# Four equal stages with 2 KB rows, the last t of the third and fourth in two parts, low parts on DVE

## The reference

```python
h = jax.nn.sigmoid(jnp.einsum('bts,st->bs', x, W1) + b1)
return h @ W2.T + b2
```

## Time and profile before

| what | before |
|---|---|
| median of 3 runs | 311.82 us |
| the profiled execution | 311.89 us |
| its span | 310.1 us |
| PE busy | 257.8 us (83%) |
| DVE busy | 246.4 us (79%) |
| POOL busy | 215.2 us (69%) |
| ACT busy | 50.9 us (16%) |
| loads and stores | 109.48 MB, mean 353 GB/s |

### The profile page before, as it was taken

One profiled execution on the slowest core, in us unless ns is written; L12 is line 12 of the kernel. 1 busy time (PEld: TensorE's weight loads), 2 busy tenths in 40 slices (PEclk: granted clock), 3 DMA queues, 4 the chain that ended last, 5 costly groups with the idle time before them and its releaser, 6 DMA issues.

```text
span 310.1 us, 4779 instructions
## 1 busy us (share of the span) xinstructions
PE 257.8 (83%) x1761; PEld 220.0 (71%) x1761; DVE 246.4 (79%) x368; ACT 50.9 (16%) x85; POOL 215.2 (69%) x125
## 2 busy tenths in 40 slices
PE   0947678648888999999579999937999988999894
PEld 0846677647766888889468887835888885888783
DVE  0729899829998978889977987877878898798865
ACT  4211223203253100100420000040101104000120
POOL 3119676626379999995799977479988848999000
PEclk9979999959999999999999999999999999999999
DMA  7999999999999999999999999999999999999007
GB/s 223 398 390 385 387 385 386 402 387 388 385 387 384 387 386 388 386 385 384 373 374 374 385 381 381 381 385 373 373 373 373 370 359 340 339 349 332 29 2 272
DMA packets 67675, 109.48 MB, mean 353 GB/s; under 512 B 3642, under 2 KB 40514, under 8 KB 67652
## 3 DMA queue, kind: packets, MB, share of 16 engines
q1 hardware_dynamic: 67056, 107.06, 96.8%
q10 hardware_dynamic: 596, 2.11, 1.7%
HBM read 104.97 MB, written 4.19 MB: 352 GB/s over the span
## 4 chain that ended last, share of the span: by engine, by line
PE 51%; DMA 31%; DVE 7%; issue 5%; ACT 3%; SPq 1%; DVEq 0%; ACTq 0%
DMA ring<-in_r_x 31%; PE xbank L232 25%; PE pbank L301 20%; DVE acc L354 4%; PE xbank L332 3%; ACT h L431 2%; DVE w_lo L361 2%; ACT h_hi L456 1%; PE pbank L291 1%; PE pbank L332 1%; PE pbank L261 0%; DVE acc L352 0%; ACT L431 0%; SPq L195 0%; SPq L201 0%
## 5 line engine op out<-in xcount | busy, mean ns | idle before, releaser
L354 DVE SCALAR_TENSOR_TENSOR acc<-xbank,w,acc 128x512 f32<-128x512 f32 x280 | 200.0, 746 | 41.1 <-PE xbank L232 35.6
L232 PE MATMUL xbank<-ident,ring 128*128 128x128 f32 x1184 | 171.5, 279 | 44.2 <-DMA ring<-in_r_x 36.0
L232 PEld LDWEIGHTS xbank<-ident,ring 128*128 128x128 f32 x1184 | 142.2, 144 | 75.7 <-issue 27.9
L485 POOL TENSOR_TENSOR nat<-nat,w1all 128x768 f32<-128x768 f32 (+2 forms) x56 | 107.2, 1916 | 60.6 <-DMA nat<-in_r_x 47.1
L495 POOL TENSOR_TENSOR nat<-nat 128x768 f32<-128x768 f32 (+2 forms) x46 | 87.8, 1908 | 3.6
L301 PE MATMUL pbank<-w_hi,h_hi 128*128 128x512 f32 x112 | 48.2, 431 | 0.3 <-ACT h_hi L456 0.2
L301 PE MATMUL pbank<-w_lo,h_hi 128*128 128x512 f32 x112 | 48.3, 432 | 0.0
L301 PE MATMUL pbank<-w_hi,h_lo 128*128 128x512 f32 x112 | 40.5, 431 | 0.0
L431 ACT ACTIVATE h<-acc,b1col 128x512 f32<-128x512 f32 (+1 forms) x22 | 12.5, 599 | 96.1 <-DVE acc L354 64.0
L443 ACT COPY y<-pbank 128x512 f32<-128x512 f32 x16 | 9.4, 587 | 79.4 <-PE pbank L301 79.4
L301 PEld LDWEIGHTS pbank<-w_hi,h_hi 128*128 128x128 f32 x112 | 21.3, 191 | 1.4 <-ACT h_hi L456 1.0
(11 more groups left out here) (37 smaller groups left out, 93.1 us busy)
## 6 DMA issues: line engine op xcount, KB each, us to landing
ring<-in_r_x SPq DMA_DIRECT2D x38, 1024.0 KB, 13.4
ring<-in_r_x SPq DMA_DIRECT2D x36, 768.0 KB, 11.1
nat<-in_r_x SPq DMA_DIRECT2D x20, 512.0 KB, 13.1
nat<-in_r_x SPq DMA_DIRECT2D x24, 384.0 KB, 11.5
ring<-in_r_x SPq DMA_DIRECT2D x18, 512.0 KB, 7.8
y<-in_L_rec_W SPq DMA_DIRECT2D x2, 2048.0 KB, 14.9
nat<-in_r_x SPq DMA_DIRECT2D x12, 256.0 KB, 8.7
out_y<-y ACTq DMA_DIRECT2D x4, 512.0 KB, 6.6
```

The source lines that it names most:

```text
L232: mm = pe.transpose(xbank[u % XBANKS][:, j * P:(j + 1) * P], tile, ident[:, :])
L354: nc.vector.scalar_tensor_tensor(out=total, in0=bank, scalar=weight, in1=total, op0=ALU.mult, op1=ALU.add).then_inc(unit_added, 1)
L485: nc.gpsimd.tensor_tensor(slot, slot, row, ALU.mult).then_inc(nat_weighed, 1)
```

## The change

`STAGES` has four stages of four chunks each, so that every load has rows of 2 KB. The pools are 4, 6, 6, 6. In the third stage the last 6 t, and in the fourth the last 10 t, come in two parts of rows: first row tiles 0 and 1 of all of those t, then row tiles 2 and 3 of all of them. Such a half load has 512 KB; two share a slot of the ring, and a half unit has two transposes and is 128 x 256 for DVE. The "n" units of these stages come in halves too. When the first part is done, its sums are complete for half of the rows, and their sigmoid, high and low parts are made while the second part is turned. For the fourth stage, the product of the first two row tiles (4 outs) begins beside the turns of the second part, and after the last turn there are 12 steps left of it and then four outs of 12 matmuls, out by out. `steps_due` counts steps over the whole kernel by STRETCHES, in proportion to tiles turned. DVE makes the low parts in place of POOL, at four places (every second unit) after each stage and each first part. ACT makes each half's sigmoids after the outs due by then were kept, and issues its stores two tiles at a time.

```diff
 STAGES = (
-    (0, 0, 4, 4, (2, 3, 5, 7, 9, 11, 13, 15, 17, 18), "keep"),
-    (0, 4, 4, 6, (0, 2, 3, 5, 6, 8, 9, 11, 12, 14, 15, 17), "last"),
-    (4, 0, 3, 6, (0, 2, 3, 5, 6, 8, 9, 11, 12, 14, 15, 17), "keep"),
-    (4, 3, 3, 6, (0, 2, 3, 5, 6, 8, 9, 11, 12, 14, 15, 17), "add"),
-    (4, 6, 2, 6, (0, 2, 3, 5, 6, 8, 9, 11, 12, 13), "last"),
+    (0, 0, 4, 0, (2, 3, 5, 7, 9, 11, 13, 15, 17, 18), "keep"),
+    (0, 4, 6, 0, (0, 2, 3, 5, 6, 8, 9, 11, 12, 14, 15, 17), "last"),
+    (4, 0, 6, 6, (0, 2, 3, 5, 6, 8, 9, 11, 12, 14, 18, 20, 21, 23), "keep"),
+    (4, 4, 6, 10, (1, 3, 4, 6, 7, 9, 11, 13), "last"),
 )
+CUT = 2
+NC = 4
...
+    loads = [[(t, 0, JT) for t in range(pools[i], T - splits[i])] for i in range(NS)]
+    for i in range(NS):
+        loads[i] += [(t, *half) for half in halves[i] for t in range(T - splits[i], T) if splits[i]]
...
+        for t, row, n in loads[i]:
+            if t == T - 2:
+                order += [("n", 0, c, row, n) for c in range(NC)]
+            order += [("x", t, c, row, n) for c in range(NC)]
...
+        AHEAD = 16
+        LATE = 8
+        HEAD = OH * CUT * steps_of(LAST)
+        STRETCHES = (
+            (OUTS * steps_of(0), first_unit[1] + 2 * NC, first_unit[1] + len(units[1]) * 4 // 5),
+            (OUTS * steps_of(1), first_unit[2] + 2 * NC, part_end(2) + NC),
+            (AHEAD, part_end(2) + 2 * NC, first_unit[3]),
+            (OUTS * steps_of(2) - AHEAD - LATE, first_unit[3], part_end(3)),
+            (LATE, part_end(3), part_end(3) + 2 * NC),
+            (HEAD - REST, part_end(3) + 2 * NC, UNITS),
+        )
...
-                    q = item_of[i, pools[i] + at]
-                    if q >= RING:
-                        sp.wait_ge(unit_turned, item_end[q - RING] + 1)
-                    sp.dma_start(ring[:, q % RING, :, :n * P],
+                    use, sub, _ = held[i, t, row]
+                    if use >= RING and sub == 0:
+                        sp.wait_ge(unit_turned, use_end[use - RING] + 1)
+                    sp.dma_start(ring[:, use % RING, sub * n:(sub + 1) * n, :],
...
+                bank, total = xbank[u % XBANKS][:, :n * P], acc[:, c, row * P:(row + n) * P]
...
+            def low_part(i, p):
+                c, row, n = sums[i][p]
+                rows = slice(row * P, (row + n) * P)
+                dve.wait_ge(h_hi_ready, first_sum[i] + p + 1)
+                nc.vector.tensor_tensor(h_lo[:, c, rows], h[:, c, rows], h_hi[:, c, rows].bitcast(F32),
+                                        ALU.subtract).then_inc(h_lo_ready, 1)
...
+            for n in range(OH * CUT, OUTS):
+                j, cols = out_half(n)
+                bank = xbank[(UNITS + n - OH * CUT) % XBANKS]
+                pe.wait_ge(unit_added, UNITS - XBANKS + n - OH * CUT + 1)
+                for c in range(NC):
                     if n % OH == 0:
-                        pe.wait_ge(tail_lo, c * JT + j + 1)
+                        pe.wait_ge(tail_lo, sum_of(LAST, c, j) - TAIL + 1)
...
+                    if u in lows:
+                        low_part(*lows[u])
...
-            def low_parts(i):
-                for c in range(chunks[i]):
-                    pool.wait_ge(h_hi_ready, first_h[i] + c + 1)
```

More of the change, by code:

```diff
@@ L58, in rec_kernel @@
     UNITS = sum(len(o) for o in units)
-    first_h = [sum(chunks[:i]) for i in range(NS)]
+    sums = [[(c, *half) for half in halves[i] for c in range(NC)] for i in range(NS)]
+    sums[LAST] = [(c, 0, CUT) for c in range(NC)] + [(c, j, 1) for j in range(CUT, JT) for c in range(NC)]
+    first_sum = [sum(len(o) for o in sums[:i]) for i in range(NS)]
+    TAIL = NC
     OUTS = OH * JT
@@ L155, in steps_of, with part_end, steps_due, steps_to @@
         def steps_of(i):
[L157 to L172, removed]
+            return 3 * NC + (fate[i] == "keep")
+        def part_end(i):
+            return first_unit[i] + max(v for v, u in enumerate(units[i]) if u[3] == 0) + 1
+        AHEAD = 16
[9 more added lines that the diff above has]
+        )
+        tiles_to = [0]
+        for order in units:
+            for unit in order:
+                tiles_to.append(tiles_to[-1] + unit[4])
+        def steps_due(u):
+            due = 0
+            for steps, a, b in STRETCHES:
+                if u >= a:
+                    due += -(-steps * (tiles_to[min(u + 1, b)] - tiles_to[a]) // (tiles_to[b] - tiles_to[a]))
+            return due
+        def steps_to(outs):
+            return sum(steps_of(g // OUTS) for g in range(outs))
+        def out_end(g):
+            i, n = divmod(g, OUTS)
+            if any(n == OH * row for row, _ in halves[i]):
+                return steps_to(g + 1) + 2 * NC + (fate[i] == "keep")
+            return steps_to(g + 1)
+        def outs_due(u):
+            return sum(out_end(g) <= steps_due(u) for g in range((NS - 1) * OUTS + OH * CUT))
         EARLY, SETN = 1 + NK0, 1 + 2 * NK
@@ L185, in _ @@
             m = 0
-            for i, (j0, c0, n, _, places, _) in enumerate(STAGES):
-                for at in range(T - pools[i]):
+            for i, (j0, c0, _, _, places, _) in enumerate(STAGES):
+                for at, (t, row, n) in enumerate(loads[i]):
                     if at in places:
@@ L218, in turn_unit @@
                 u = first_unit[i] + v
-                kind, t, c = units[i][v]
+                kind, t, c, row, n = units[i][v]
                 if u >= XBANKS:
@@ L431, in sigmoid @@
+            def sigmoid(i, p):
+                c, row, n = sums[i][p]
+                rows = slice(row * P, (row + n) * P)
+                act.wait_ge(unit_added, sum_end(i, p))
                 nc.scalar.activation(h[:, c, rows], acc[:, c, rows], ACT.Sigmoid,
                                      bias=b1col[:, bass.ds(STAGES[i][1] + c, 1)]).then_inc(h_ready, 1)
+                if i < LAST or p < TAIL:
+                    act.wait_ge(h_ready, first_sum[i] + p + 1)
+                    nc.scalar.copy(h_hi[:, c, rows], h[:, c, rows]).then_inc(h_hi_ready, 1)
@@ L444, in _ @@
[L444 to L459 removed]
+                for half, (row, n) in enumerate(halves[i]):
+                    if i == 2 and half == 0:
+                        store_tile(0)
+                        store_tile(1)
+                    if i == 3 and half == 0:
+                        store_tile(2)
+                        store_tile(3)
+                    part = [p for p, s in enumerate(sums[i]) if row <= s[1] < row + n]
+                    outs = outs_due(sum_end(i, part[0]) - 1)
+                    for g in range(kept, outs):
+                        if fate[g // OUTS] == "keep":
+                            keep_out(g // OUTS, g % OUTS)
+                    kept = outs
+                    if i > 0:
+                        act.wait_ge(h_lo_ready, min(first_sum[i], first_sum[LAST]))
+                        act.wait_ge(out_summed, OUTS * (i - 1) + OH * (row + n))
+                    for p in part:
+                        sigmoid(i, p)
```

251 lines of the change are left out of this document (124 added, 127 removed).

## The result

The changed kernel takes 314.07 us (median of 4 runs, 313.76 to 318.29) against 311.78 us (4 runs): 0.7% slower by the medians. The ratio of the mean times is 1.010, with a 95% interval of 1.0069 to 1.0131; the one run of 318.29 us raises the ratio and widens its interval. The profiled execution took 314.37 us, with a span of 312.5.

The account below looks back on a forecast made before the run. Loads and PE were both taken as near their bound. Landing at 262.9 plus 29.9 of PE work gave the last turn at 292.9; 18.0 of tail made span 310.9, time 312.6 us, own range 311.5 to 313.8, whole range 309.9 to 315.5.

Parts of the forecast that it names:

- rival B: On PE, a half unit with one step takes 0.50 us, not 0.466: time 314.7; chance 0.22.
- wrong altogether: Sign: GB/s well under 386 before 280 us, or PE idle on h_hi or h_lo at the second part's start.
- landing of t = 19: Last stage's sixth half load, the last with a POOL load ahead of it, lands at 262.9 us.
- edit (1): DVE's extra work: 72 more units 8.6 us, 20 low parts 8.8 us, mostly under the loads outside the last part.
- edit 5: Last stage's ring holds 5 MiB, not 2.5; PE may lag some 11 us, so no gap in the loads.
- Rival D: Store cost beside reads moves the landings 1 us each way: last turn as much later, only 0.8 us earlier.
- rival A: On PE, half unit plus step takes 0.38 us, not 0.466, and DVE decides: time 309.9; chance 0.24.
- rival C: DVE's half units cost full duration, 0.480 us for 256 columns, not 0.39: time 316.4; chance 0.10.
- The tail: After the last turn: 18.0 us against 19.2 before, as PE's 1.2 us gap goes; 4.07 from last add to end.
- The stage turns (3): At a stage's turn, DVE's first multiply waits for its chunk's sigmoid as before; the loads cover it.
- SP's number of loads (4): SP issues 90 ring loads and 44 for POOL, before 92 and 56: zero cost.
- POOL (2): POOL loses 14 low parts, 17.7 us, and isn't late with its 44 parts: zero cost.

Follow-up runs that it names:

- e1: Changed kernel with 16 of its 20 low parts made by POOL, the last four still on DVE: 312.80 us, 1.003 to the kernel before.
- e2: Kernel before the change with only its 14 low parts moved from POOL to DVE: 312.16 us, 1.0009 to the kernel before.
- e3: Changed kernel with POOL's instructions 16 of each 512 columns wide, most work on its sums left out: 312.81 us, 1.0031 to the kernel before.
- e8: Changed kernel with 16 low parts on POOL and the third stage in one part, its product wholly in the last stage: 314.66 us.
- e9: Changed kernel with all low parts on POOL, third-stage steps earlier, and the last stage's last 8 t in two parts, not 10: 312.55 us.
- e11: Changed kernel with all low parts on POOL, third-stage steps earlier, and 12 of the last stage's t in two parts, not 10: 310.54 us.
- e10: Changed kernel with the low part as h times a constant, one SBUF input in place of two: 314.74 us, one run.

## Why the prediction came out as it did

The forecast was 312.6, slower by 0.25%; measured were 314.07, slower by 0.7%. The direction was right and the size a third. The forecast's own range ended at 313.8, and the measured time lies between it and rival B's 314.7, though B didn't come about. What did was the prediction's own sign of "wrong altogether", slices well under 386 GB/s ahead of 280 us, to which it gave 0.04. That the time is inside the whole range, 309.9 to 315.5, is therefore partly luck. The miss can be put beside the sum:

| term | forecast | changed kernel | e1 |
|---|---|---|---|
| landing of t = 19 | 262.9 | 266.25 | 264.78 |
| from PE's start on it to the last turn | 29.9 | 29.1 | 29.15 |
| last turn to the end of the span | 18.0 | 17.0 | 17.0 |
| span | 310.9 | 312.5 | 311.1 |

In both traces 13 steps follow the last turn, where the sum has 12, so 0.23 us of the third row belongs to the second; like for like PE's part was 0.5 us too long in the sum and the tail 1.2. In e1 these 1.8 us cancel a landing that is 1.9 us late: its total is right by luck, and the changed kernel's would have missed by 3.4 us without them.

- **The step that was mis-sized is edit (1), the low parts.** I took 0.60 and 0.33 us from start to start from rows in which POOL is idle (the 128-column piece at the end) or an input is in PSUM. Measured were 1665 and 1079 ns in duration, 26.3 us in all, where the sum had 8.8. I said that they lie under the loads outside the last part. In the kernel before they cost no time (e2), and in the changed one they made the hole: it is gone when they are (e1) and when POOL's instructions are short (e3).
- **"I expect no gap in the loads" (edit 5) was wrong.** I looked only at the slots of the ring. But the load for POOL waits for the last "n" units and holds the ring loads behind it, for 11.1 us here. The long low parts and the hole behind them are worth 1.3 us by e1 and e3. That this load's place has a part in it is read from the trace; another place for it was not tried.
- **The landing was 1.9 us late without the hole too.** In e1 the 27th load landed 0.3 us late already (issued at 97.30, landed at 110.2). From there to 264.78 the stream ran at 388 GB/s, no slower than in the sum, and so moved some 57.2 MiB (an estimate from rate and time) where the sum counts 56.5. So it is not the rate that was wrong but what had to move before that landing; whose bytes the 0.7 MiB are isn't settled. Rival D allowed 1 us.
- **PE's work behind the landing held.** In the changed kernel a half unit with one step takes 0.45 us (the starts of two transposes at 283.34 and 283.79), against 0.466 in the sum: neither rival A (0.38) nor B (0.50). The turn-and-step view of PE:

```profile
283.34 0.38 PE L303 MATMUL xbank<-ident,ring 128*128 128x128 f32 x2
283.47 0.48 PE L375 MATMUL pbank<-w_lo,h_hi 128*128 128x512 f32 x1
283.79 0.38 PE L303 MATMUL xbank<-ident,ring 128*128 128x128 f32 x2
```

- **DVE's half units held** (rival C fell): eight in 3.22 us with 475 ns for one are 0.39 from start to start. Of the two rules of the Trainium skill that the prediction cites (VectorE: DVE Perf Modes, the section on the errata and "The DRAIN you can't avoid"), the trace agrees with the fixed part of each small tile (2 x 0.39 is 0.12 more than 0.66) and not with the wait for an empty pipe.
- **The tail held but for the last store.** The gap before the product went. From the last add's start to the end are 3.1 us where I kept 4.07: the last adds, and so the last stores, are now 2.7 us apart, while before all eight stores were issued within 5.1 us. That the one explains the other is argued, not tried.
- **The stage turns (3) and SP's number of loads (4)** cost nothing that e1 shows. Nor does POOL (2), even with 16 low parts given back to it.

## What to carry to other kernels

Before an elementwise instruction is moved to DVE, look at what POOL does at that moment and whether the instruction has an input in PSUM: beside POOL's 2.4 us instructions, one without took two to three times its time, and rows with POOL idle don't show it. A faster load stream moves the bound to whatever work may only begin late; here the splits that let steps start earlier gained more than their fixed parts cost (e8, e9, e11), though why was read and not tried. A schedule edit is to be tried after the stall ahead of it is gone: the same 15 steps moved cost 2.0 us with the hole and gained 0.7 without.

## What the runs showed of the hardware

The low part, an f32 instruction of DVE from SBUF to SBUF, was held beside POOL's 128 x 1024 instructions with two inputs and with one (e10): it took up to 2.6 us where the subtraction takes 0.41 (256 columns) or 0.68 (512) undisturbed. When it meets one, it ends a fixed time after it, 0.55 us for 512 columns and 0.28 for 256, and about half of that with one input, so the two take turns and don't share. Instructions with one input in PSUM don't change (L421's kind 679 ns before and after, L423's 746 and 742). POOL's weighing grew too, from 2382 to 2413 ns on average, and the one begun at 96.80, while a low part still ran, took 2.83 us. And PE's granted clock went to 0.50 at 220 to 228 us, after PE had been busy for 1.6 us of 4 waiting for banks, and was back at 1.00 only from 232 on. A step took 0.78 us there and 0.48 after it, so a stall of PE also makes the work behind it slower.
